# A four-stage model on one core: the next stage's weights, their preparations, the position shift and the turn of the expert loop

## The chip, the cores and the metric

One core of a Trainium2 chip runs one kernel. The metric is the device time of a run in microseconds (us), and the number given for a kernel is the median of its runs. The engines are PE (TensorE), DVE (VectorE), ACT (ScalarE), POOL (GpSimd) and SP (SyncE, which here only issues transfers).

## What is computed

A sequence model of two layers on x of 16 x 256 tokens by 128. Each stage is followed by x + stage(x) and a layer norm:

```python
x = _layernorm(x + _L0_attn_ref(x, ...))   # 16 heads of 64, j < i + 64; keys, queries, values from an MLP
x = _layernorm(x + _L0_ffn_ref(x, ...))    # 16 experts, 4 chosen per token
x = _layernorm(x + _L1_attn_ref(x, ...))   # 16 heads of 8; every weight W has a LoRA part A, B
x = _layernorm(x + _L1_ffn_ref(x, ...))    # a gated recurrence over 32 steps, as a scan over the batches
```

The expert stage and the LoRA part of the next one are what the change touches:

```python
logits = -sum((x - keys) ** 2) + x @ rw.T + rb
topv, topi = top_k(logits, 4); w = softmax(topv)
fused = sum(w * (gelu(x @ w1[e].T + b1[e]) @ w2[e].T + b2[e]) for e in topi)
y = x @ W.T + x @ A.T @ Blo.T / 16          # q, k, v and the output of the second attention
```

## The kernel before

The program gives each engine its own list of instructions, written out by hand; semaphores join them. It has four parts in time.

**First attention**, to 698 us. Batches 0 to 15 run through a loop (`batch_loop`, line 38: two turns written out, a `Fori` loop, the last turns written out). Towards a batch's end the router picks four experts for each token, and VectorE works out in which row of the DRAM array `xs` each token's copy goes: `posf_all` keeps the position of each of the 128 x 128 (token, choice) pairs, counted as if each expert had CAP rows. GpSimd scatters the tokens there (L493, eight indirect transfers a batch).

**The join.** When the last batch is counted, VectorE makes the plan: `NT` = 144 tiles of 128 rows, for each tile the expert and its first row. SP stores it and loads it back as one row, SP and ACT write zero rows behind each expert's tokens (`pad`, L353), PE multiplies the second bias out (L789). All four compute engines then meet at `a_done` (L507, L790 and their like; GpSimd counts itself there only after its scatters). Arrays of the first attention end here, and those of the later stages take their place in SBUF; `cw`, `lora_a`, `lora_b`, `gw`, `gu`, `gcol`, `bo1`, `bo2` are among these.

**Expert tiles**, from 712 us. [...] All five engines go round four tiles a turn. VectorE's order in a tile:

```python
e = expert_of(n + 2)       # a register read from the plan
need(dve, "hid_ready", 4 * n - 4)
weights_A(e, q)            # wA of tile n + 2
rows_T(n + 2, q)           # xgT of tile n + 2
v.tensor_tensor(yrow[:, m, :], DN[p % 2][:, 0:D], ...)   # tile n - 2
weights_B(e, q)            # wB of tile n + 2
```

Into the second written-out turn is put work for the later stages. SP issues eight loads after its first turn (L362). PE, ahead of tile 4, waits for all eight and multiplies the LoRA factors (L808); `add_lora` (L1312, L1314) adds them to `cw`; at tile 5 PE waits for that (`c_set`). After turn 1, `prepare` (L1319 to L1327) makes the small constants of the last stage on VectorE, and compares each position with the first row of each of the 16 experts (`shift`, 128 x 128 x 16). GpSimd waits for that compare (`plan_ready` 3), multiplies by `delta`, by how much an expert's rows move when the experts are packed without gaps (L534), adds the 16 up (L538, four sums of halves), adds the result to the positions (L541, L543), and goes on to clear and fill `qst`, `kst` and `v32` for the second attention (L511 to L553).

**Second attention with the recurrence**, from 1030 us, in one loop of three batches a turn; GpSimd gathers the rows of `ys` for it (L567).

Of the kernel before, what the change touches and what calls it, by code (L numbers as in the profile page):

```python
# [7 lines left out]
ACT = mybir.ActivationFunctionType  # L8
# [4 lines left out]
TT = N // 128  # L13
# [18 lines left out]
NT += -NT % 4  # L32
# [66 lines left out]
def build(nc, t, out):  # L99
    ctx = ExitStack()  # L100
    with ctx:
# [245 lines left out]
        def is_tile(i, p, off):  # L347
            return 0 <= 4 * i + p + off < NT if isinstance(i, int) else True
# [10 lines left out]
        def _(sp):  # L359
# [14 lines left out]

            sp.wait_ge(s["plan_ready"], 1)
# [31 lines left out]
            def body(i):  # L407
                for p in range(4):
                    n = 4 * i + p
                    if is_tile(i, p, 4):  # L410
                        load_rows(n + 4, p)
                    if p % 2 == 1 and is_tile(i, p, -5):
                        store_rows(n - 5, (p - 5) % 4)
                if isinstance(i, int) and i == 0:
                    for dst, src in ((cw, "cw"), (lora_a, "lora_a"), (lora_b, "lora_b"), (gw, "gw"), (gu, "gu"), (gcol, "gcol"),
                                     (bo1, "bo1"), (bo2, "bo2")):
                        load(dst, src, "cw_in")

            batch_loop(sp, 2, NT // 4 - 1, 2, body)
# [31 lines left out]
        def _(pool):  # L451
# [79 lines left out]
            pool.wait_ge(s["plan_ready"], 3)  # L531

            at = posf_all[:, :].rearrange("q (n o) -> q n o", o=1)
            g.tensor_tensor(shift[:, :, :], shift[:, :, :], delta[:, :].rearrange("q (o e) -> q o e", o=1).to_broadcast([128, npos, E]), ALU.mult)  # L534
            g.drain()
# [99 lines left out]
        def _(pe):  # L635
# [903 lines left out]
```

## Time and profile before

| what | us |
|---|---|
| three runs: 1596.56, 1600.42, 1598.92; median | 1598.92 |
| the profiled execution's own time | 1603.28 |
| its span | 1601.5 |
| PE busy in the span | 1305.1 (81%) |
| VectorE | 1059.0 (66%) |
| ScalarE | 960.6 (60%) |
| GpSimd | 785.4 (49%) |

Times in the profile count from the start of the span. "L818" is line 818 of the kernel as printed above. A row names the engine, the operation and its tiles as out<-in. Buffer numbers are left out, and an array seen through another one's memory has that one's name: `shift` shows as `qst`, `v32` as `v`. SPq, DVEq and POOLq are the engines' sequencers. The busy shares are averages over stages with different limits, so they don't tell what a change in one stage is worth; the idle time in brackets, and what ended it, do.

### The profile page before, as it was taken

The numbers are of one execution on the slowest core, as the hardware profiler recorded it, in microseconds if no ns is written. First come the engines' busy times: TensorE is split into PE (matmuls) and PEld (weight loads), VectorE is DVE, ScalarE is ACT, GpSimd is POOL, SyncE is SP. The second block draws the span as 40 slices with busy tenths as digits, with TensorE's granted clock in tenths as the row PEclk, the third lists the DMA queues.
The fourth block names the chain that finished last, engine by engine and source line by source line (L and its number), as shares of the span: only waits on it lengthen the run. The fifth ranks groups of instructions, "written<-read, shape, count | busy, mean of one in ns | idle before, by whom it ended". The sixth has DMA issues, their size and how long they took to land.

```text
span 1601.5 us, 37212 instructions
## 1 busy us (share of the span) xinstructions
PE 1305.1 (81%) x9486; PEld 975.0 (61%) x9486; DVE 1059.0 (66%) x3801; ACT 960.6 (60%) x2716; POOL 785.4 (49%) x898
## 2 busy tenths in 40 slices
PE   7999999999999999746799999703778777787871
PEld 3766666666666666436799999602445445455540
DVE  1677777777777777637766666414776767777646
ACT  5877777777777777423455555302565656556654
POOL 1567777777777777624400000276656655652003
PEclk9999999999999999958999999956898989889986
DMA  9100000000000000021122222123423223232101
GB/s 343 45 8 16 13 11 13 13 13 13 13 13 13 13 13 14 16 66 55 49 66 66 66 66 66 54 50 54 81 49 77 54 51 75 46 72 43 31 0 53
DMA packets 77063, 75.02 MB, mean 47 GB/s; under 512 B 10913, under 2 KB 66977, under 8 KB 75330
## 3 DMA queue, kind: packets, MB, share of 16 engines
q1 hardware_dynamic: 67506, 56.86, 13.9%
q0 software_dynamic: 8192, 16.79, 3.8%
q10 hardware_dynamic: 1296, 0.59, 0.1%
q8 instruction: 26, 0.43, 0.1%
q14 instruction: 43, 0.35, 0.1%
HBM read 46.87 MB, written 27.33 MB: 46 GB/s over the span
## 4 chain that ended last, share of the span: by engine, by line
PE 32%; issue 6%; ACT 5%; DVE 5%; POOL 3%; DVEq 2%; POOLq 2%; SPq 1%; DMA 0%; ACTq 0%
PE psum L818 8%; PE psum L829 7%; PE psum L862 3%; PE psum L851 3%; PE psum L926 3%; POOL yk L567 2%; ACT qst L1098 2%; PE psum L942 2%; PE psum L943 1%; ACT wall L1054 1%; ACT wall L1098 1%; DVE wA L1292 1%; PE psum L798 1%; PE psum L884 1%; DVEq L1431 1%
## 5 line engine op out<-in xcount | busy, mean ns | idle before, releaser
L503 POOL TENSOR_SCALAR P<-P,rinv 128x192 f32<-128x192 f32 (+1 forms) x384 | 308.8, 818 | 164.4 <-DVE rinv L1170 162.7
L1010 ACT ACTIVATE P<-shifted,least 128x192 f32<-128x192 f32 (+1 forms) x512 | 240.2, 471 | 126.4 <-DVE least L1156 125.1
L1044 ACT ACTIVATE hid<-psum,wA 128x128 f32<-128x128 f32 x576 | 164.9, 369 | 146.8 <-PE psum L818 146.7
L1368 DVE TENSOR_REDUCE mx<-psum 128x2 f32<-128x512 f32 x256 | 164.4, 685 | 82.6 <-PE psum L926 79.2
L1156 DVE CUSTOM_DVE_ANT_0 shifted<-psum,band 128x192 f32<-128x192 f32 (+1 forms) x512 | 168.7, 384 | 30.5 <-PE psum L695 30.2
L1054 ACT ACTIVATE wall<-psum 128x1024 f32<-128x1024 f32 x128 | 131.2, 1025 | 83.5 <-PE psum L851 81.2
L818 PE MATMUL psum<-xgT,wA 128*128 128x128 f32 x1152 | 162.3, 285 | 18.0 <-DVE xgT L1299 16.3
L818 PEld LDWEIGHTS psum<-xgT,wA 128*128 128x128 f32 x1152 | 143.7, 196 | 25.6 <-issue 25.3
L493 POOL DMA_INDIRECT xs<-x1c,pos x128 | 128.0, 1000 | 55.9 <-issue 28.2
L829 PE MATMUL psum<-wB,hid 128*128 128x128 f32 x1152 | 154.0, 278 | 0.0
L567 POOL DMA_INDIRECT yk<-ys,posc x128 | 123.7, 967 | 49.5 <-issue 37.1
L829 PEld LDWEIGHTS psum<-wB,hid 128*128 128x128 f32 x1152 | 142.1, 194 | 0.0
L731 PEld LDWEIGHTS psum<-ident,P 128*128 128x128 f32 x1024 | 116.8, 141 | 35.9 <-issue 28.9
L731 PE MATMUL psum<-ident,P 128*128 128x128 f32 x1024 | 134.1, 274 | 3.5 <-POOL P L503 1.4
L695 PE MATMUL psum<-kT,qT 64*128 64x192 f32 (+1 forms) x1024 | 131.5, 375 | 0.6 <-DVE least L1156 0.6
L1292 DVE COPY wA<-wall 128x516 f32 x144 | 75.4, 523 | 77.6 <-ACT hid L1044 67.4
L511 POOL MEMSET wall<- 128x2048 f32 x1 | 1.8, 1809 | 247.6 <-DVE wB L1295 247.6
L749 PE MATMUL psum<-PT,V 128*64 128x256 f32 (+1 forms) x1024 | 112.5, 362 | 0.7 <-DVE PT L1144 0.7
L695 PEld LDWEIGHTS psum<-kT,qT 64*128 64x128 f32 x1024 | 80.2, 186 | 38.5 <-issue 37.2
L1010 ACT ACTIVATION_READ_ACCUMULATOR P<-shifted,least 128x1 f32 x512 | 95.9, 187 | 0.0
L1295 DVE COPY wB<-wall 128x640 f32 x144 | 82.1, 570 | 19.8
L646 PE MATMUL psum<-hT,wg 128*128 (+1 forms) x256 | 88.9, 429 | 0.9 <-ACT kT L967 0.9
(247 smaller groups left out, 2671.8 us busy)
## 6 DMA issues: line engine op xcount, KB each, us to landing
xg<-xs SPq DMA_DIRECT2D x144, 64.0 KB, 1.8
ys<-yrow SPq DMA_DIRECT2D x72, 128.0 KB, 1.9
wall<-in_wall SPq DMA_DIRECT2D x1, 8232.0 KB, 36.6
qkd<-parts SPq DMA_DIRECT2D x32, 192.0 KB
qst<-qkd SPq DMA_DIRECT2D x66, 64.0 KB
wall<-qkd SPq DMA_DIRECT2D x35, 64.0 KB
kst<-qkd SPq DMA_DIRECT2D x11, 192.0 KB
hT<-in_xT SPq DMA_DIRECT2D x4, 512.0 KB, 6.1
```

Of the source, the lines that this page charges most:

```text
L493: nc.gpsimd.indirect_dma_start(out=xs, out_offset=bass.IndirectOffsetOnAxis(pos[:, k:k + 1], 0), in_=x1c[:, k // TOPK, :], in_offset=None) ...
L503: g.tensor_scalar(x, x, rinv[:, par, n:n + 1], None, ALU.mult).then_inc(s["pn_ready"], 1)
L567: g.indirect_dma_start(out=yk[:, n, :], out_offset=None, in_=ys, in_offset=bass.IndirectOffsetOnAxis(posc[:, n:n + 1], 0)).then_inc(s["yk_ ...
L695: last = mm(bk[:, c0:c0 + w], qT[64 * h:64 * h + 64, p, it * 128:(it + 1) * 128], kT[64 * h:64 * h + 64, p, 0:w], start=True, stop=True)
L731: last = nc.tensor.transpose(bk[:, c0:c0 + 128], P[:, par1, it, h, jt * 128:(jt + 1) * 128], ident[:, :])
L818: mm(UP[two][:, at:at + GT], wA[:, p, f * 128:(f + 1) * 128], xgT[:, p, :], start=True, stop=True).then_inc(s["up_mm"], 1)
L829: last = mm(DN[two][:, 0:D], hid[:, m, f, :], wB[:, m, f * D:(f + 1) * D], start=(f == 0), stop=(f == FC - 1))
L1010: last = sc.activation(P[:, par, it, h, 0:w], shifted[:, par, it, h, 0:w], ACT.Exp, scale=-1.0, bias=least[:, par, n:n + 1], accum_out=row ...
L1044: sc.activation(hid[:, p, f, :], UP[two][:, at:at + GT], ACT.Gelu, bias=wA[:, p, F + f:F + f + 1]).then_inc(s["hid_ready"], 1)
L1054: sc.activation(pc[:, p % 4, :, :, :].rearrange("q h j n -> q (h j n)"), ST, ACT.Exp, scale=SCALE1).then_inc(s["exps1"], 1)
L1156: v.tensor_tensor_reduce(out=shifted[:, par, it, h, 0:w], in0=bk[:, c0:c0 + w], in1=band[:, it, 0:w], scale=-SCALE0, scalar=3.0e38, op0=AL ...
L1368: v.tensor_reduce(out=mx[:, :, h], in_=SB[(par + 1 + h) % 3].rearrange("q (i n) -> q i n", i=TT), axis=mybir.AxisListType.X, op=ALU.max).t ...
```

## The change

It touches nothing that is computed. Five things:

- SP issues the eight loads right after the last output product of the first attention (`wo_mm`), ahead of the plan's store.
- PE multiplies the LoRA factors after the bias products, ahead of the join; VectorE adds them to `cw` after the plan, ahead of the join. No wait for them is left among the tiles.
- VectorE makes the last stage's constants right after the join, ahead of the first `wA`.
- The compare and the product of the position shift become 16 instructions on GpSimd, one per expert, each (position >= first row) x delta; GpSimd no longer waits for VectorE there.
- A turn of the expert loop has eight tiles (`TURN`) on every engine. `NT` stays 144. 16 tiles in front and 8 behind are written out in place of 8 and 4, and 15 turns are left of 33.

The diff, without the places where 4 becomes `TURN` in ACT's loop and in `is_tile`:

```diff
 DUMMY = E * CAP
 NT = (TOK * TOPK + E * (GT - 1)) // GT
-NT += -NT % 4
+TURN = 8
+NT += -NT % TURN
 ROWS = DUMMY + GT
...
+            sp.wait_ge(s["wo_mm"], PAIRS * B)
+            for dst, src in ((cw, "cw"), (lora_a, "lora_a"), (lora_b, "lora_b"), (gw, "gw"), (gu, "gu"), (gcol, "gcol"), (bo1, "bo1"), (bo2, "bo2")):
+                load(dst, src, "cw_in")
             sp.wait_ge(s["plan_ready"], 1)
...
             def body(i):
-                for p in range(4):
-                    n = 4 * i + p
+                for p in range(TURN):
+                    n = TURN * i + p
                     if is_tile(i, p, 4):
-                        load_rows(n + 4, p)
+                        load_rows(n + 4, p % 4)
                     if p % 2 == 1 and is_tile(i, p, -5):
                         store_rows(n - 5, (p - 5) % 4)
-                if isinstance(i, int) and i == 0:
-                    for dst, src in ((cw, "cw"), (lora_a, "lora_a"), (lora_b, "lora_b"), (gw, "gw"), (gu, "gu"), (gcol, "gcol"),
-                                     (bo1, "bo1"), (bo2, "bo2")):
-                        load(dst, src, "cw_in")
-
-            batch_loop(sp, 2, NT // 4 - 1, 2, body)
+
+            batch_loop(sp, 2, NT // TURN - 1, 2, body)
...
-            pool.wait_ge(s["plan_ready"], 3)
+            pool.wait_ge(s["plan_ready"], 2)
+            for e in range(E):
+                g.tensor_scalar(shift[:, :, e], posf_all[:, :], first_row[:, e:e + 1], delta[:, e:e + 1], ALU.is_ge, ALU.mult)
+            g.drain()
             at = posf_all[:, :].rearrange("q (n o) -> q n o", o=1)
-            g.tensor_tensor(shift[:, :, :], shift[:, :, :], delta[:, :].rearrange("q (o e) -> q o e", o=1).to_broadcast([128, npos, E]), ALU.mult)
-            g.drain()
...
+            pe.wait_ge(s["cw_in"], 128)
+            pe.wait_ge(s["pos_ready"], B)
+            for k in range(4):
+                last = mm(MIS[1][:, k * D:(k + 1) * D], lora_a[:, k, :], lora_b[:, k, :], start=True, stop=True)
+            last.then_inc(s["lora_mm"], 1)
...
             rows_in(0, 0, 16)
+            pe.wait_ge(s["c_set"], 1)
             rows_in(1, 1, 16)
             def tiles(i):
-                if isinstance(i, int) and i == 1:
-                    pe.wait_ge(s["cw_in"], 128)
-                    pe.wait_ge(s["xgT_ready"], 6)
-                    for k in range(4):
-                        last = mm(MIS[1][:, k * D:(k + 1) * D], lora_a[:, k, :], lora_b[:, k, :], start=True, stop=True)
-                    last.then_inc(s["lora_mm"], 1)
-                for p in range(4):
-                    n, two = 4 * i + p, p % 2
+                for p in range(TURN):
+                    n, two = TURN * i + p, p % 2
                     if is_tile(i, p, 0):
...
                             at = (f // 2) * 512 + (f % 2) * GT
-                            mm(UP[two][:, at:at + GT], wA[:, p, f * 128:(f + 1) * 128], xgT[:, p, :], start=True, stop=True).then_inc(s["up_mm"], 1)
-                    if isinstance(i, int) and i == 1 and p == 1:
-                        pe.wait_ge(s["c_set"], 1)
+                            mm(UP[two][:, at:at + GT], wA[:, p % 4, f * 128:(f + 1) * 128], xgT[:, p % 4, :], start=True, stop=True).then_inc(s["up_mm"], 1)
                     if is_tile(i, p, 2):
-                        rows_in(n + 2, (p + 2) % 4, 16 * (i + (p + 2) // 4) + 16)
+                        rows_in(n + 2, (p + 2) % 4, 16 * (i * (TURN // 4) + (p + 2) // 4) + 16)
...
+            dve.wait_ge(s["lora_mm"], 1)
+            for k in range(2):
+                v.scalar_tensor_tensor(cwqk[:, k, :].rearrange("q (d h) -> q h d", h=H1), MIS[1][:, k * D:(k + 1) * D].rearrange("q (h d) -> q h d", h=H1), LORA,
+                                       cw[:, k, :].rearrange("q (h d) -> q h d", h=H1), ALU.mult, ALU.add)
+            v.scalar_tensor_tensor(cw[:, 2:4, :], MIS[1][:, 2 * D:4 * D].rearrange("q (k d) -> q k d", k=2), LORA, cw[:, 2:4, :], ALU.mult, ALU.add)
+            v.drain().then_inc(s["c_set"], 1)
             dve.wait_ge(s["wall_in"], 16)
             dve.wait_ge(s["a_done"], 4)
+            v.tensor_copy(identb[:, :], ident[:, :])
+            v.tensor_scalar(gu[:, :, :], gu[:, :, :], 0.5, None, ALU.mult)
+            v.tensor_scalar(gcol[:, 0:2], gcol[:, 0:2], 0.5, None, ALU.mult)
+            v.memset(c2[:, :], 0.0)
+            v.drain()
+            v.tensor_scalar(c2[:, :], c2[:, :], gcol[:, 3:4], 2.0, ALU.add, ALU.mult).then_inc(s["scan_done"], 1)
...
-            def add_lora():
...
-                npos = B * TT * TOPK
-                v.tensor_tensor(shift[:, :, :], posf_all[:, :].rearrange("q (n o) -> q n o", o=1).to_broadcast([128, npos, E]),
-                                first_row[:, :].rearrange("q (o e) -> q o e", o=1).to_broadcast([128, npos, E]), ALU.is_ge).then_inc(s["plan_ready"], 1)
             def tiles(i):
-                for p in range(4):
-                    n, q = 4 * i + p, (p + 2) % 4
-                    if isinstance(i, int) and i == 1 and p == 0:
-                        add_lora()
+                for p in range(TURN):
+                    n, q = TURN * i + p, (p + 2) % 4
...
-                if isinstance(i, int) and i == 1:
-                    prepare()
-            batch_loop(dve, 2, NT // 4 - 1, 2, tiles)
+            batch_loop(dve, 2, NT // TURN - 1, 2, tiles)
```

How the order of instructions moves at three places (lines are those of each version). **PE at the join**, before: the bias products (the source is in `wall`) and then the first transposes of tiles (`xg`), with no LoRA product before tile 4.

```order
L789 MATMUL psum<-ident,wall 128x128 [waits wall_in]
L789 MATMUL psum<-ident,wall 128x128 x15
L798 MATMUL psum<-ident,xg 128x128 [waits xg_in0,a_done]
L798 MATMUL psum<-ident,xg 128x128 [waits xg_in1]
L818 MATMUL psum<-xgT,wA 128x128 [waits wA_ready,xgT_ready]
```

and now, on PE at the same place:

```order
L790 MATMUL psum<-ident,wall 128x128 x15
L794 MATMUL psum<-lora_b,lora_a 128x128 [waits pos_ready,cw_in]
L794 MATMUL psum<-lora_b,lora_a 128x128 x3
L804 MATMUL psum<-ident,xg 128x128 [waits xg_in0,a_done]
L804 MATMUL psum<-ident,xg 128x128 [waits xg_in1,c_set]
```

The four LoRA products stand ahead of the wait for `a_done`, and wait for the loads and for the last positions. **VectorE at the join**, before: the last value of the plan (`delta`), then the first expert's number and the first `wA`.

```order
L1279 COPY delta<-past 128x1
L1280 TENSOR_TENSOR delta<-past 128x15
L1289 TENSOR_LOAD plan [waits plan_in,a_done,wall_in]
L1289 ISA x2
L1292 ISA
L1292 COPY wA<-wall 128x516
```

and now, on VectorE at the same place (`c` is `c2`):

```order
L1278 TENSOR_TENSOR delta<-past 128x15
L1282 SCALAR_TENSOR_TENSOR cwqk<-psum,cw 128x16x8 [waits lora_mm]
L1282 SCALAR_TENSOR_TENSOR cwqk<-psum,cw 128x16x8
L1284 SCALAR_TENSOR_TENSOR cw<-psum,cw 128x256
L1290 CAST identb<-ident 128x128 [waits a_done,wall_in]
L1291 TENSOR_SCALAR gu<-gu 128x512
L1292 TENSOR_SCALAR gcol<-gcol 128x2
L1293 MEMSET c 128x256
L1295 TENSOR_SCALAR c<-c,gcol 128x256
L1300 TENSOR_LOAD plan [waits plan_in]
```

Three instructions came in ahead of the join and five between it and the first expert's number. **GpSimd after the join**, before, and now:

```order
L534 TENSOR_TENSOR qst<-qst,delta 128x2048 [waits scat,plan_ready,a_done]
L538 TENSOR_TENSOR qst<-qst 128x128x8
L538 TENSOR_TENSOR qst<-qst 128x128x4
L538 TENSOR_TENSOR qst<-qst 128x128x2
L538 TENSOR_TENSOR qst<-qst 128x128
```

```order
L534 TENSOR_SCALAR qst<-posf_all,first_row,delta 128x128 [waits scat,plan_ready,a_done]
L534 TENSOR_SCALAR qst<-posf_all,first_row,delta 128x128 x15
L539 TENSOR_TENSOR qst<-qst 128x128x8
L539 TENSOR_TENSOR qst<-qst 128x128x4
L539 TENSOR_TENSOR qst<-qst 128x128x2
```

One instruction over 2048 columns became 16 over 128, and what follows them is the same. The `plan_ready` it waits for is now the plan's own, no longer the compare's.

## Rows read from the trace of the kernel before

**Rows 1.** Busy time by engine in two stretches (start:end us, length, busy, PEclk, DMA)

```profile
698.00:712.60 14.60, 0.45 (x1) 0.18 (x1) 0.61 (x3) 0.00 (x0) 4.42 (x5) 0.55 0.37 110
...
738.07:780.82 42.75, 26.50 (x189) 25.09 (x188) 40.56 (x46) 12.91 (x44) 35.04 (x20) 0.88 0.12 34
```

**Rows 2.** In order of time (start us, us, engine line operation), tile 3 to tile 6

```profile
718.35 0.43 SPq L362 DMA_DIRECT2D cw<-in_cw  x1
...
718.93 1.06 PE L818 MATMUL psum<-xgT,wA 128*128 128x128 f32 x8
...
722.19 0.91 SPq L362 DMA_DIRECT2D bo<-in_bo  x2
...
725.08 2.07 PE L808 MATMUL psum<-lora_b,lora_a 16*128 16x128 f32 x8 [4.09 <-DMA bo<-in_bo]
...
727.26 0.59 DVE L1312 SCALAR_TENSOR_TENSOR cwqk<-psum,cw 128x128 f32<-128x128 f32 x2 [5.31 <-PE psum L808]
...
732.40 1.06 PE L818 MATMUL psum<-xgT,wA 128*128 128x128 f32 x8
```

**Rows 3.** In order of time, from the second turn's end to the end of GpSimd's chain

```profile
737.23 0.22 DVE L1319 CAST identb<-ident 128x128 bf16<-128x128 f32 x1
...
738.08 1.06 PE L818 MATMUL psum<-xgT,wA 128*128 128x128 f32 x8
...
738.48 2.28 DVE L1327 TENSOR_TENSOR qst<-posf_all,first_row 128x2048 f32<-128x2048 f32 x1
...
740.92 4.55 POOL L534 TENSOR_TENSOR qst<-qst,delta 128x2048 f32<-128x2048 f32 x1 [37.27 <-DVE qst L1327]
...
762.69 1.96 POOL L521 TENSOR_SCALAR_AFFINE_SELECT kst<-kst 24x2048 bf16<-24x2048 bf16 x1 [0.19 <-issue]
...
762.78 2.16 DVE L1292 COPY wA<-wall 128x516 f32 x1
...
778.35 0.36 POOL L553 MEMSET v<- 128x96 f32 x1
```

**Rows 4.** Up-projections over one turn, and VectorE's branches (durations ns min/median/max)

```profile
856.51 1.15 PE L818 MATMUL psum<-xgT,wA 128*128 128x128 f32 x8
...
860.43 1.08 PE L818 MATMUL psum<-xgT,wA 128*128 128x128 f32 x8
...
862.34 1.07 PE L818 MATMUL psum<-xgT,wA 128*128 128x128 f32 x8
...
864.48 1.15 PE L818 MATMUL psum<-xgT,wA 128*128 128x128 f32 x8
...
L43 DVEq COMPARE_BRANCH  x46: 50/56/72, 147.0 to 1021.8; - x46
```

**Rows 5.** The join: instructions in order of time, and two waits by line

```profile
674.87 1.13 PE L711 MATMUL psum<-OT,wo 128*128 128x256 f32 x4 [0.84 <-DVE OT L1148]
...
682.57 0.96 POOL L493 DMA_INDIRECT xs<-x1c,pos  x1 [0.30 <-issue]
...
690.77 6.28 PE L789 MATMUL psum<-ident,wall 128*128 128x128 f32 x32
...
707.51 0.43 DVE L1292 COPY wA<-wall 128x516 f32 x1 [9.33 <-issue]
...
712.62 0.29 DVE L1299 COPY xgT<-psum 128x128 f32<-128x128 f32 x1 [4.69 <-PE psum L798]
...
L507 POOLq DRAIN  x1: 1293/1293/1293, 705.1 to 705.1; - x1
...
L388 SPq EVENT_SEMAPHORE  x1: 1177/1177/1177, 707.6 to 707.6; - x1
```

**Rows 6.** Groups of GpSimd by line and shape (xcount | busy us, mean ns | idle)

```profile
L503 POOL TENSOR_SCALAR P<-P,rinv 128x192 f32<-128x192 f32 x256 | 196.0, 766 | 164.4 <-DVE rinv L1170 162.7
...
L503 POOL TENSOR_SCALAR P<-P,rinv 128x256 f32<-128x256 f32 x128 | 118.1, 923 | 0.0
...
L576 POOL TENSOR_TENSOR rstd<-ve,minus_half 128x4 f32<-128x4 f32 x12 | 12.5, 1043 | 44.5 <-DVE ve L86 44.4
```

More of the change, by code:

```diff
@@ L347, in is_tile @@
         def is_tile(i, p, off):
-            return 0 <= 4 * i + p + off < NT if isinstance(i, int) else True
+            return 0 <= TURN * i + p + off < NT if isinstance(i, int) else True
         def pad(eng, e):
@@ L830, in tiles @@
                         last.then_inc(s["dn_mm"], 1)
-            batch_loop(pe, 2, NT // 4 - 1, 2, tiles)
+            batch_loop(pe, 2, NT // TURN - 1, 2, tiles)
             pe.wait_ge(s["c_set"], 1)
@@ L1036, in tiles @@
             def tiles(i):
-                for p in range(4):
-                    n, two = 4 * i + p, p % 2
+                for p in range(TURN):
+                    n, two = TURN * i + p, p % 2
                     if is_tile(i, p, 0):
@@ L1043, in tiles @@
                             need(act, "up_mm", 4 * n + (2 * (f // 2) + 2))
-                            sc.activation(hid[:, p, f, :], UP[two][:, at:at + GT], ACT.Gelu, bias=wA[:, p, F + f:F + f + 1]).then_inc(s["hid_ready"], 1)
-            batch_loop(act, 2, NT // 4 - 1, 2, tiles)
+                            sc.activation(hid[:, p % 4, f, :], UP[two][:, at:at + GT], ACT.Gelu, bias=wA[:, p % 4, F + f:F + f + 1]).then_inc(s["hid_ready"], 1)
+            batch_loop(act, 2, NT // TURN - 1, 2, tiles)
             def attention(b, par):
@@ L1305, in _ @@
                 weights_B(first, n)
-            def add_lora():
-                dve.wait_ge(s["cw_in"], 128)
-                dve.wait_ge(s["lora_mm"], 1)
-                for k in range(2):
-                    v.scalar_tensor_tensor(cwqk[:, k, :].rearrange("q (d h) -> q h d", h=H1), MIS[1][:, k * D:(k + 1) * D].rearrange("q (h d) -> q h d", h=H1), LORA,
-                                           cw[:, k, :].rearrange("q (h d) -> q h d", h=H1), ALU.mult, ALU.add)
-                v.scalar_tensor_tensor(cw[:, 2:4, :], MIS[1][:, 2 * D:4 * D].rearrange("q (k d) -> q k d", k=2), LORA, cw[:, 2:4, :], ALU.mult, ALU.add)
-                v.drain().then_inc(s["c_set"], 1)
-            def prepare():
-                v.tensor_copy(identb[:, :], ident[:, :])
-                v.tensor_scalar(gu[:, :, :], gu[:, :, :], 0.5, None, ALU.mult)
-                v.tensor_scalar(gcol[:, 0:2], gcol[:, 0:2], 0.5, None, ALU.mult)
-                v.memset(c2[:, :], 0.0)
-                v.drain()
-                v.tensor_scalar(c2[:, :], c2[:, :], gcol[:, 3:4], 2.0, ALU.add, ALU.mult).then_inc(s["scan_done"], 1)
-                npos = B * TT * TOPK
-                v.tensor_tensor(shift[:, :, :], posf_all[:, :].rearrange("q (n o) -> q n o", o=1).to_broadcast([128, npos, E]),
-                                first_row[:, :].rearrange("q (o e) -> q o e", o=1).to_broadcast([128, npos, E]), ALU.is_ge).then_inc(s["plan_ready"], 1)
             def tiles(i):
-                for p in range(4):
-                    n, q = 4 * i + p, (p + 2) % 4
-                    if isinstance(i, int) and i == 1 and p == 0:
-                        add_lora()
+                for p in range(TURN):
+                    n, q = TURN * i + p, (p + 2) % 4
                     if is_tile(i, p, 2):
```

2 lines of the change are left out of this document (1 added, 1 removed).

## The prediction

> **What bounds the kernel now.** The stretch to read is the expert stage with the join ahead of it. I took the stages first [rows 1], then the instructions in order of time. From 698 to 712.6 us the join holds all engines: PE runs one matmul in 14.6 us and the clock averages 0.55. Then 144 tiles follow. Three things there set the time.
>
> First, a hole after tile 3 [rows 2]. Tile 3's up-projection starts at 718.93, and PE then waits for the eight loads that SP issues from 718.35 (the two bo, last, from 722.19 to 723.10). The LoRA products run only at 725.08, and tile 6 starts at 732.40: 13.47 us for three tiles.
>
> Second, GpSimd's chain [rows 3]. From VectorE's compare at 738.48 to GpSimd's last memset at 778.71, tiles are slow: 42.75 us [rows 1] for 11 tiles (the stage's two ends are put where up-projections start, the 1st and the 12th). The reader is to see why in one pair of rows: beside a GpSimd select of 1.96 us, the copy of wA takes 2.16 us, where it takes 0.43 us alone [rows 5]. The copy stands still until GpSimd's instruction is over, and a tile has two such copies.
>
> Third, the turn of the loop [rows 4]. In the quiet part after the chain, a turn takes 864.48 - 856.51 = 7.97 us, 1.99 us a tile. Inside it one tile takes 862.34 - 860.43 = 1.91 us, so four make 7.64 us, and 0.33 us is the turn's own. It falls on VectorE, whose branch, register work and read of the next expert's number delay the copies for which PE waits.
>
> **The change, part by part.**
>
> *The hole after tile 3.* Unrolled tiles are 1.89 us apart ((738.08 - 732.40) / 3 [rows 2, 3]). Without the loads and the products, three tiles take 5.68 us in place of 13.47: **-7.8 us**. What moves must be hidden elsewhere. The eight issues take SP 4.75 us (718.35 to 723.10 [rows 2]); they start when the last output product is done, at 674.87 + 1.13 = 676.0 [rows 5], so SP is free again near 681. Behind them in SP's queue stands the store of the plan, which VectorE can't have ready before the bias products' start at 690.77 [rows 5], since it counts the last batch first. What could suffer is GpSimd's scatter, with its last issue of that batch at 682.57 [rows 5], for which VectorE waits before it writes x1c: 0 to +1 us, taken as 0, since the loads are issued before. The four LoRA products cost PE 2.07 us [rows 2] after the bias products, which end at 690.77 + 6.28 = 697.05: PE is through at about 699.2, and VectorE's additions follow (two take 0.59 us [rows 2], a third comes) to about 700.2. The join opens only when GpSimd's drain ends, at 705.1 + 1.29 = 706.4 [rows 5]. Cover: 6 us; without it, 3 us would be paid.
>
> *Preparations ahead of tile 0.* VectorE's five small instructions take 738.48 - 737.23 = 1.25 us [rows 3]. They stand behind the join and push the first wA copy from 707.51 to about 708.8, or 711 if each waits for one of GpSimd's. PE cannot use it before xgT of tile 0, at 712.62, because SP first waits for the padding rows until 707.6 + 1.18 = 708.8 [rows 5]. Cost 0; up to +1 if the cover breaks.
>
> *Positions on GpSimd.* The compare of 2.28 us on VectorE and the product of 4.55 us on GpSimd go [rows 3]; 16 GpSimd instructions over 128 columns come. No row shows such a compare there. The nearest row is the same operation with a column as its scalar: 192 columns take 766 ns, 256 take 923 ns [rows 6], so 2.45 ns a column and, at 128, about 610 ns: 9.8 us in all. Bounds: 766 - 192 x 2.45 = 296 ns (4.7 us) is the part that doesn't depend on columns; upward 923 ns (14.8 us), if the second scalar costs as much as the columns saved. The far bound is the power, 1043 ns for 4 columns [rows 6]; I leave it to a rival, since it is another kind of function and the scale is the same kind of instruction. The Trainium skill speaks against this move: "GPSIMD Engine Reference", section "Performance versus the Vector engine", puts elementwise work on GpSimd at 1.96 times VectorE's time and keeps it on VectorE. By it the compare of 2.28 us would become 4.5 us, 5.3 us less than my 9.8; the end would be about 1 us earlier than below.
>
> *Where the chain now lies.* It starts at 706.4 in place of 738.48. The rest of it, from 745.47 (the product's end) to 778.71, is 33.2 us and stays. The small instructions end at 706.4 + 9.8 = 716.2, the rest at about 749.5. The 11 slow tiles cost 42.75 - 11 x 1.99 = 20.9 us, over 40.2 us of chain 0.52 us a microsecond. Afterwards the 33.2 us cost the same share, 17.3 us; of the small ones only 712.6 to 716.2 lies beside tiles, two tiles whose copies wait at most 0.6 us each, say 1.0 us. So 18.3 in place of 20.9: **-2.6 us**. Bounds: +3 (longer small instructions, and a clock that stays at 1.2 GHz under the holes; it averaged 0.88 in that stretch [rows 1]), and -6 (the first blocks fall on tiles that PE runs slowly anyway).
>
> *Eight tiles a turn.* 33 turns become 15: 18 x 0.33 = 5.9 us; 12 more tiles are unrolled at 1.89 instead of 1.91: 0.2 us. **-6.1 us**. Bounds -4 to -6.5: the branch row shows VectorE's at 50 to 72 ns over loops of different length [rows 4], so a longer body should cost nothing or little.
>
> Sum: -7.8 - 2.6 - 6.1 = -16.5 us. The profiled execution took 1603.3 us (span 1601.5), 4.4 above the median of 1598.9; against the median, 1582.4 us, so **1582 us**.
>
> **The rivals.**
>
> *A heavier front (18%).* The compare costs 923 ns or more, the holes of GpSimd's chain start while the clock is low, and it stays low through them. Then the second term is +3 and the loop gives 5: -7.8 + 3 - 5 = -9.8, about 1589 us. For it: the clock at 0.55 before tile 0. Against it: over the old chain it averaged 0.88.
>
> *A lighter front (12%).* The chain's blocks fall where PE is slow anyway and where the pipeline fills: -7.8 - 6 - 6.5 = -20.3, about 1578.5 us. For it: PE's first groups after the join run at the low clock. Against it: VectorE is then the later one all the same.
>
> *The longer turn saves nothing (5%).* The turn's cost grows with its body, so half the turns at twice the cost: -10.4, about 1588.5 us. Against it: the branch's 50 to 72 ns [rows 4]. The Trainium skill, "Runtime: NRT & Kernel Launch", section "Instruction fetch mechanics", says that a taken branch to code outside the window of two pages must fetch it first; a turn of eight tiles would do so if its code outgrew that window. No row shows such a stall.
>
> *Slower: the compare is dear (4%).* If one of the 16 took t us, the chain would be 16 x (t - 0.61) longer, all of it beside tiles that then take two instructions each. At t = 3: 38.2 us more, of which 1 - 1.91 / 6.2 is lost: +26.4, so about 1609 us, slower than before. It decides from t = 2.4 on (28.6 us x 0.62 = 17.7, more than the 16.5 won). For it: the power row, over 200 ns a column. Against it: the product ran at 4.55 us for 2048 columns [rows 3], 2.2 ns each, and the scale at 2.45.
>
> *The hole only moves (3%).* If the loads disturb the scatter and the LoRA products come after the drain, 6 us of the first term return: 1588 us; with the heavy front as well, about 1596 us, no change.
>
> **How the numbers follow.** The forecast has 58%. About 0.2%, 3.2 us, is what a measurement of this kernel can tell from no change. All cases but the dear compare and the double misfortune lie below 1595.7: faster 0.92, same 0.04, slower 0.04. The range takes in the unknowns of the forecast and both fronts, 1578.5 to 1589, with 2 us either way for the medians (the three runs before spread over 3.9): 1576 to 1591.
>
> **What would show it.** Tile 4's up-projection 1.9 to 4 us after tile 3's, and no LoRA row between them. GpSimd's 16 rows at about 0.6 us from 706 on, its last memset near 750, wA and wB copies of about 2 us between 722 and 750 and none later. Tile 0 still at 713. In the quiet part, eight tiles in 15.6 us. The tile stage 16.5 us shorter, and the second attention moved as a whole. Wrong it would be if tile 0 came late, if a compare took over 1 us, or if a turn took 15.9 us.

## The result and the profile after

The changed kernel takes 1579.85 us (median of four runs, 1579.33 to 1581.43), beside 1599.67 for the kernel before on the same chip (four runs, 1596.56 to 1603.67): a ratio of 0.988, 95% interval 0.986 to 0.990. Forecast were 1582.0 us and a range of 1576 to 1591. So it is 1.2% faster, and 2.2 us below the forecast. In what follows "the stage" is the time from the first to the last up-projection of the expert tiles.

A tile goes through the engines like this (lines of the changed kernel). SP loads its 128 rows into `xg`, PE transposes them (L804), and VectorE copies the result to `xgT` (L1310). VectorE also copies the expert's weights out of `wall` to `wA` (L1303) and `wB` (L1306). PE's up-projection (L818) reads `wA` and `xgT`, ScalarE applies the gelu (L1042), PE's down-projection (L827) reads `wB` two tiles later, VectorE adds the bias (`yrow`, L1331), and SP stores the rows.

| | before | after | change |
|---|---|---|---|
| profiled execution, its own time | 1603.28 | 1580.31 | -22.97 |
| span | 1601.5 | 1578.5 | -23.0 |
| start of tile 0's up-projection | 713.23 | 714.78 | +1.55 |
| the stage, first to last up-projection | 312.33 | 293.87 | -18.46 |
| from there to the end | 575.96 | 569.89 | -6.07 |

The last row has no edit in it (the experiments come back to it). Two stretches, the join and what follows to the end of GpSimd's chain, by engine with the columns of [rows 1]:

```profile
698.00:712.60 14.60, 1.18 (x9) 0.96 (x8) 3.54 (x15) 0.58 (x1) 10.15 (x12) 0.58 0.35 105
712.60:756.50 43.90, 31.64 (x224) 29.57 (x224) 39.08 (x54) 17.17 (x57) 41.11 (x30) 0.87 0.16 46
```

GpSimd works through both; before, it was idle in the first 28 us of the tiles. The second line answers to the second of [rows 1], where 11 tiles took 42.75 us; now 14 tiles take 41.74 us, from 714.78 to 756.52. The first six of these are quick, and the slow ones lie behind them. The join in order of time, against [rows 5]:

```profile
675.90 1.13 PE L712 MATMUL psum<-OT,wo 128*128 128x256 f32 x4 [0.84 <-DVE OT L1146]
...
677.06 0.34 SPq L363 DMA_DIRECT2D cw<-in_cw  x1
...
679.82 0.91 SPq L363 DMA_DIRECT2D bo<-in_bo  x2
...
691.91 6.18 PE L790 MATMUL psum<-ident,wall 128*128 128x128 f32 x32
...
698.02 1.15 PE L794 MATMUL psum<-lora_b,lora_a 16*128 16x128 f32 x8
...
699.25 0.58 DVE L1282 SCALAR_TENSOR_TENSOR cwqk<-psum,cw 128x128 f32<-128x128 f32 x2
...
707.58 0.23 DVE L1290 CAST identb<-ident 128x128 bf16<-128x128 f32 x1 [7.50 <-POOLq L507]
707.71 15.67 POOL L534 TENSOR_SCALAR qst<-posf_all,first_row,delta 128x128 f32<-128x128 f32 x16 [2.92 <-POOLq L507]
...
713.94 0.29 DVE L1310 COPY xgT<-psum 128x128 f32<-128x128 f32 x1 [3.82 <-PE psum L804]
...
714.78 1.94 PE L818 MATMUL psum<-xgT,wA 128*128 128x128 f32 x8
```

The reader is to see three things. The loads, the LoRA products and their additions are over at about 700.1, while VectorE waits 7.50 us for GpSimd's drain: they are covered. The whole join is about 1 us later than before, but so is its first row, the last output product (675.90 against 674.87), which comes ahead of every edit. And the 16 compares take 15.67 us, 0.98 us each, where 0.61 was forecast. (Their group in the profile has a mean of one of 1069 ns, since neighbours overlap.) Next, tiles 3 to 5 and the chain beside the tiles, against [rows 2, 3]:

```profile
720.49 1.06 PE L818 MATMUL psum<-xgT,wA 128*128 128x128 f32 x8
...
722.39 1.06 PE L818 MATMUL psum<-xgT,wA 128*128 128x128 f32 x8
...
724.28 1.06 PE L818 MATMUL psum<-xgT,wA 128*128 128x128 f32 x8
...
740.46 1.96 POOL L521 TENSOR_SCALAR_AFFINE_SELECT kst<-kst 24x2048 bf16<-24x2048 bf16 x1 [0.19 <-issue]
740.54 2.16 DVE L1303 COPY wA<-wall 128x516 f32 x1
...
742.95 1.16 PE L818 MATMUL psum<-xgT,wA 128*128 128x128 f32 x8 [2.15 <-DVE xgT L1310]
...
747.22 1.32 PE L818 MATMUL psum<-xgT,wA 128*128 128x128 f32 x8 [2.11 <-DVE xgT L1310]
...
756.11 0.36 POOL L554 MEMSET v<- 128x96 f32 x1
```

Tiles 3, 4 and 5 are 1.9 us apart: the hole is gone. Beside the selects a tile takes 747.22 - 742.95 = 4.27 us, as before, with the same 2.16 us copy. The chain ends at 756.47 where 749.5 was forecast. Last, a turn of the loop in the quiet part, the first up-projection of two turns in a row, against [rows 4]:

```profile
858.23 1.15 PE L818 MATMUL psum<-xgT,wA 128*128 128x128 f32 x8 [0.16 <-DVE xgT L1310]
...
873.94 1.15 PE L818 MATMUL psum<-xgT,wA 128*128 128x128 f32 x8 [0.16 <-DVE xgT L1310]
```

Eight tiles take 15.71 us. At 1.91 each they make 15.28, and 0.43 us is the turn's own, where 0.33 was forecast.

The stage's -18.46 us splits by the differences between up-projections: the three tiles of the hole -7.8, counted as what they took above 1.9 us each; the slow tiles beside GpSimd's chain, summed over what each takes above 1.9 us, 21.85 before and 15.24 after, -6.6; the same sum over the rest of the stage 11.0 and 6.94, -4.1.

### The profile page after: what moved, and what is told of

The parts are those of the page before. It is cut to its first block, busy times and chain, and to the rows that moved or that the text cites. A ratio compares the mean times of both kernels' runs of the same rounds, so it can differ in the third digit from the quotient of the medians.

```text
span 1578.5 us, 36791 instructions
## 1 busy us (share of the span) xinstructions
PE 1297.7 (82%) x9486; PEld 970.0 (61%) x9486; DVE 1055.8 (67%) x3800; ACT 959.6 (61%) x2716; POOL 796.1 (50%) x913
## 3 DMA queue, kind: packets, MB, share of 16 engines
q1 hardware_dynamic: 67506, 56.86, 14.1%
## 4 chain that ended last, share of the span: by engine, by line
PE 30%; issue 6%; DVE 6%; ACT 6%; DVEq 3%; POOL 2%; POOLq 1%; SPq 1%; DMA 0%; ACTq 0%
PE psum L818 7%; PE psum L827 6%; PE psum L860 4%; PE psum L849 3%; PE psum L924 3%; ACT qst L1096 2%; POOL yk L568 2%; PE psum L940 2%; PE psum L941 1%; ACT wall L1052 1%; DVE wA L1303 1%; ACT wall L1096 1%; PE psum L882 1%; PE psum L804 1%; DVE xgT L1310 1%
## 5 line engine op out<-in xcount | busy, mean ns | idle before, releaser
L1042 ACT ACTIVATE hid<-psum,wA 128x128 f32<-128x128 f32 x576 | 164.1, 368 | 129.2 <-PE psum L818 129.1
L818 PE MATMUL psum<-xgT,wA 128*128 128x128 f32 x1152 | 158.4, 281 | 13.0 <-DVE xgT L1310 12.3
L827 PE MATMUL psum<-wB,hid 128*128 128x128 f32 x1152 | 153.3, 277 | 0.0
L818 PEld LDWEIGHTS psum<-xgT,wA 128*128 128x128 f32 x1152 | 141.6, 193 | 17.4 <-DVE xgT L1310 12.1
L827 PEld LDWEIGHTS psum<-wB,hid 128*128 128x128 f32 x1152 | 141.4, 194 | 0.0
L732 PEld LDWEIGHTS psum<-ident,P 128*128 128x128 f32 x1024 | 116.8, 141 | 36.2 <-issue 29.3
L1303 DVE COPY wA<-wall 128x516 f32 x144 | 75.7, 526 | 64.1 <-ACT hid L1042 57.0
L1306 DVE COPY wB<-wall 128x640 f32 x144 | 79.1, 549 | 19.9
```

The lines of the kernel that those rows point to most:

```text
L732: last = nc.tensor.transpose(bk[:, c0:c0 + 128], P[:, par1, it, h, jt * 128:(jt + 1) * 128], ident[:, :])
L818: mm(UP[two][:, at:at + GT], wA[:, p % 4, f * 128:(f + 1) * 128], xgT[:, p % 4, :], start=True, stop=True).then_inc(s["up_mm"], 1)
L827: last = mm(DN[two][:, 0:D], hid[:, m, f, :], wB[:, m, f * D:(f + 1) * D], start=(f == 0), stop=(f == FC - 1))
L1042: sc.activation(hid[:, p % 4, f, :], UP[two][:, at:at + GT], ACT.Gelu, bias=wA[:, p % 4, F + f:F + f + 1]).then_inc(s["hid_ready"], 1)
```

## The experiments

Every kernel was measured beside the kernel before on the same chip. The stage of the kernel before was 312.33 and 313.93 us in its two profiles, 313.1 in the mean, against which the second column is taken.

| kernel | stage | less 313.1 | median less that of before | ratio, 95% interval |
|---|---|---|---|---|
| changed | 293.87 | -19.2 | -19.8 | 0.986 to 0.990 |
| changed, second time | 293.25 | -19.9 | -19.3 | 0.986 to 0.991 |
| changed, third time | 293.45 | -19.7 | -24.3 | 0.984 to 0.988 |
| changed, 4 tiles a turn | 298.49 | -14.6 | -22.1 | 0.985 to 0.991 |
| the same, second time | 299.10 | -14.0 | -16.6 | 0.988 to 0.991 |
| changed, 16 tiles a turn | 289.81 | -23.3 | -21.1 | 0.982 to 0.987 |
| before + early loads | 304.73 | -8.4 | -6.8 | 0.995 to 0.998 |
| before + compares on GpSimd | 306.29 | -6.8 | -9.4 | 0.993 to 0.996 |
| changed, GpSimd's chain in halves | 286.13 | -27.0 | -29.4 | 0.980 to 0.985 |
| changed, chain in quarters | 281.19 | -31.9 | -32.5 | 0.977 to 0.981 |
| quarters, 4 tiles a turn | 286.74 | -26.4 | -30.9 | 0.980 to 0.983 |
| quarters, 16 tiles a turn | 276.92 | -36.2 | -36.6 | 0.976 to 0.980 |

### The changed kernel once more

> The changed kernel once more. In the two profiles the expert stage (first to last up-projection) took 312.3 us before and 293.9 us changed, and from the last up-projection to the end it took 575.9 before and 569.8 changed, although nothing there was edited. Theory A (that part varies by itself): the stage is again 293.9 within 0.5 us, while the part behind it differs from 569.8 by more than 1 us. Rival B (the 6 us belong to the change, by where the gathers fall): 569.8 within 1 us again.

Measured: 1580.30 us (six runs, 1574.86 to 1583.44) beside 1599.55, and a stage of 293.25 us. The stage repeats within 0.7 us, a little more than the 0.5 expected, single runs of the whole within some 9. The part behind the stage took 567.96 us against 569.89, so it varies by more than 1 us with the same kernel: theory A.

### Four tiles a turn

```diff
-TURN = 8
+TURN = 4
```

> The changed kernel with four tiles a turn. By the two traces the quiet part costs 1.99 us a tile with four a turn and 1.964 with eight. Theory A: the loop gave 4 to 5 us, so this is 4 to 5 us slower than the changed kernel, the first 15 tiles unchanged. Rival B (a longer turn costs in proportion to its body): under 1 us slower.

Measured: a stage of 298.49 us, 5.2 longer than the changed kernel's measured beside it. A turn takes 7.97 us, as in the kernel before. But the median was 1577.48 us, 2.8 **below** the changed kernel's. By the stage theory A holds, by the median rival B. The pair was run again below.

### The loads and the LoRA products alone

```diff
 # the kernel before, with
+            sp.wait_ge(s["wo_mm"], PAIRS * B)
+            for dst, src in (...): load(dst, src, "cw_in")      # all eight
 # LoRA products after the bias products, add_lora ahead of the join, no c_set wait at tile 5
```

> The kernel before, with the eight loads, the LoRA products and their additions ahead of the join, all else as before. Theory A: the hole after tile 3 closes and nothing takes its place: 7.8 us faster than before. Rival B: the hole only moves (join later, or the chain's stall deeper): under 4 us faster.

Measured: 1592.76 beside 1599.55 us, ratio 0.9963, and a stage of 304.73: -7.6 us against the first profile of before, -8.4 against the mean of two. The hole is gone, and the slow tiles beside GpSimd's chain cost what they had cost. What is left of the second obstacle stands in this kernel's trace in order of time: VectorE's compare, GpSimd's product, and what tiles 10 and 11 wait for.

```profile
730.23 2.28 DVE L1324 TENSOR_TENSOR qst<-posf_all,first_row 128x2048 f32<-128x2048 f32 x1
...
732.66 4.55 POOL L533 TENSOR_TENSOR qst<-qst,delta 128x2048 f32<-128x2048 f32 x1 [29.67 <-DVE qst L1324]
733.17 0.97 PEld L816 LDWEIGHTS psum<-xgT,wA 128*128 128x128 f32 x8 [1.47 <-issue]
733.18 1.15 PE L816 MATMUL psum<-xgT,wA 128*128 128x128 f32 x8 [1.28 <-DVE xgT L1306]
...
733.39 4.18 DVE L1302 COPY wB<-wall 128x640 f32 x1
...
737.49 2.54 DVE L1299 COPY wA<-wall 128x516 f32 x1
...
740.36 2.07 PE L816 MATMUL psum<-xgT,wA 128*128 128x128 f32 x8 [5.03 <-DVE xgT L1306]
```

The compare puts VectorE back by 2.28 us. Beside the product of 4.55 us the copy of `wB` takes 4.18 us, and beside the first of the sums that follow the copy of `wA` takes 2.54. So the up-projections at 733.18 and 740.36 are 7.18 us apart (the one before 733.18 starts at 729.84). That place cost 6.7 us above two ordinary tiles (3.34 + 7.18 - 3.8). Most of it is the compare's and the product's; VectorE's small preparations, 1.25 us just ahead of the compare, and the first sum have a part in it that no run separates. The changed kernel has neither compare nor product there, and makes its preparations ahead of tile 0.

### The compares on GpSimd alone

```diff
 # the kernel before, with
-            pool.wait_ge(s["plan_ready"], 3)
+            pool.wait_ge(s["plan_ready"], 2)
+            for e in range(E): g.tensor_scalar(shift[:, :, e], ..., ALU.is_ge, ALU.mult)
 # VectorE's compare and GpSimd's product taken out
```

> The kernel before, with the 16 compares on GpSimd right after the join (and no compare on VectorE), the loads and the LoRA products left where they were. Theory A: GpSimd's compares lie beside the join and the hole, where no tile waits for a copy; the rest of its chain costs 15 us as in the changed kernel, less what falls in the hole: 6 to 9 us faster than before. Rival B (the chain costs the same 21 us wherever it lies, and the gain of the changed kernel came from the hole and the loop): under 3 us faster.

Measured: 1590.19 beside 1599.55 us, ratio 0.9945, and a stage of 306.29, so -6.0 or -6.8. The stage lies at the lower end of the 6 to 9 us expected and the median just above it, and rival B (under 3) is out. The prediction had given this part 2.6 us. Two things that the other edits change meet here. GpSimd's sums run while PE stands in the hole anyway, which costs nothing. And VectorE's small preparations, still behind turn 1, now fall among the selects:

```profile
743.18 1.96 POOL L521 TENSOR_SCALAR_AFFINE_SELECT kst<-kst 24x2048 bf16<-24x2048 bf16 x1 [0.19 <-issue]
743.26 1.96 DVE L1320 CAST identb<-ident 128x128 bf16<-128x128 f32 x1
...
745.48 1.91 DVE L1322 TENSOR_SCALAR gcol<-gcol 128x2 f32<-128x2 f32 x1
...
752.82 1.43 PE L819 MATMUL psum<-xgT,wA 128*128 128x128 f32 x5 [8.25 <-DVE xgT L1300]
```

Three of them take 1.9 us each, 1.91 us for two columns of `gcol`, where ahead of tile 0 in the changed kernel they take 0.15 to 0.43. The up-projection at 752.82 comes 11.35 us after the last one, 7.1 more than a slow tile. Moving the preparations ahead of tile 0 keeps this from happening once the chain starts early; what it is worth alone was not tried. The three parts alone, -8.4, -6.8 and -5.3 (four tiles a turn against eight), make -20.5; the whole is -19.6 in the mean of three profiles. They add up within 1 us. That is partly luck: the free sums and the dear preparations of this kernel pull in opposite directions.

### GpSimd's chain in quarters and in halves

What costs a slow tile its time: so much for each microsecond of chain, as the prediction had it, or the length of the single GpSimd instruction that a copy waits for? These kernels do the same work on the same elements in more instructions (in quarters 4 memsets become 16, six selects 24, and so on), so the chain gets longer.

```diff
             for r in ...:
-                g.affine_select(out=r, in_=r, ..., pattern=[[-1, H1 // 2], [0, N]], ...)
+                for c in pieces(N):          # four slices
+                    g.affine_select(out=r[:, :, c], in_=r[:, :, c], ..., pattern=[[-1, H1 // 2], [0, N // 4]], ...)
```

The memsets, the copy and the larger sums are cut likewise; the compares are not.

> The changed kernel with GpSimd's chain after the compares cut up: each clear, select, copy and sum of about 2 us becomes four instructions of a quarter of the columns (the clear of v32 six), the same work in all. Theory A (a copy on VectorE stands still until the GpSimd instruction under way is over, so what counts is how long ONE of them is): beside pieces of 0.3 to 0.7 us a tile takes 1.9 to 2.3 us as it did beside the 0.94 us compares, though the chain gets some us longer; the 15 us that the chain cost fall to 2 to 5, stage 281 to 284 us instead of 293.5. Rival B (the two engines share a bandwidth, the total counts): stage within 2 us of 293.5.

> The same with halves, pieces of about 1 us. Theory A: a tile's two copies wait at most 1 us each, about as beside the compares (0.94 us): stage 283 to 287 us. If the wait grows evenly with the piece's length, half of what the chain cost remains: about 286 us. Rival B: within 2 us of 293.5.

Measured: quarters 1562.46 us (five runs, 1560.49 to 1563.47) beside 1594.93, ratio 0.979; halves 1565.55 (1561.02 to 1572.24), 0.983. The stages are 281.19 and 286.13, both in the range of theory A, where rival B had 291.5 to 295.5. The groups by line and shape (count | busy us, mean ns) show why. First the changed kernel, the copies beside the compares (715 to 723.4) and beside whole instructions (727 to 756):

```profile
L1306 DVE COPY wB<-wall 128x640 f32 x5 | 2.9, 578 | 0.3
L1303 DVE COPY wA<-wall 128x516 f32 x5 | 2.5, 493 | 0.8 <-issue 0.5 <-ACT hid L1042 0.2
...
L1303 DVE COPY wA<-wall 128x516 f32 x8 | 14.9, 1863 | 0.0
L1306 DVE COPY wB<-wall 128x640 f32 x8 | 11.4, 1425 | 1.1
```

Then the same two copies with the chain in halves (730 to 750), with its selects:

```profile
L1313 DVE COPY wA<-wall 128x516 f32 x9 | 10.3, 1149 | 0.6 <-ACT hid L1052 0.3
L1316 DVE COPY wB<-wall 128x640 f32 x8 | 5.9, 739 | 1.1
...
L527 POOL TENSOR_SCALAR_AFFINE_SELECT kst<-kst 24x1024 bf16<-24x1024 bf16 x12 | 14.0, 1188 | 1.1 <-issue 1.1
```

and in quarters (737.8 to 760):

```profile
L1316 DVE COPY wB<-wall 128x640 f32 x11 | 8.6, 781 | 1.6
L1313 DVE COPY wA<-wall 128x516 f32 x10 | 7.1, 709 | 1.7 <-ACT hid L1052 1.6
...
L527 POOL TENSOR_SCALAR_AFFINE_SELECT kst<-kst 24x512 bf16<-24x512 bf16 x24 | 18.3, 794 | 1.1 <-issue 1.1
```

and last the kernel before with GpSimd idle (856 to 880), for the four alone:

```profile
L1295 DVE COPY wB<-wall 128x640 f32 x12 | 5.9, 494 | 1.7
L1292 DVE COPY wA<-wall 128x516 f32 x13 | 5.6, 430 | 7.1 <-ACT hid L1044 7.1
L1299 DVE COPY xgT<-psum 128x128 f32<-128x128 f32 x13 | 3.7, 284 | 0.0
L1345 DVE TENSOR_TENSOR yrow<-psum,wB 128x128 f32<-128x128 f32 x12 | 3.4, 280 | 0.0
```

Alone the four make 0.56 + 0.43 + 0.49 = 1.48 us a tile, where PE takes 1.9: a slack of 0.4 us. Beside the compares they make 0.56 + 0.49 + 0.58 = 1.63 us, 2.05 beside quarters, 2.45 beside halves and 3.85 beside whole instructions. The tiles measured 1.9, then 1.9 to 2.3, then 2.4 to 2.6, then mostly 4.1 to 4.3. So **a tile takes about the larger of PE's 1.9 us and VectorE's sum**: this is a rule read off these four cases, and at whole instructions the tiles are some 0.3 us longer than the sum. GpSimd instructions that lengthen the copies by less than the slack cost nothing. The selects' own time rose from 11.7 us in six to 18.3 us in 24, the chain ended 7.9 us later (764.34 against 756.47), and the stage was 12.7 us shorter than in the first profile of the changed kernel. A price for each microsecond of chain is refuted.

The Trainium skill, "SBUF — State Buffer", section "SBUF: two separate sides", says that VectorE and GpSimd share a pair of ports by an exclusive lock: a GpSimd instruction, or a VectorE one in a two-port mode or with two inputs from SBUF, gets the pair for the whole instruction, and the other one fully blocks. The trace agrees for the selects: the copy of `wA` beside one of 1.96 us took 2.16, beside one of 0.79 us some 0.71. It does not agree for the compares, if their rows in the profile are the time for which they hold the ports: they last 0.98 us, and the copies beside them took 0.49 and 0.58, 0.06 to 0.09 more than alone. Why was not tried. So a row's length alone doesn't tell what an instruction does to VectorE: 0.98 us of compare did less than 0.79 us of select. Cutting one kind of instruction into shorter ones is shown to help; whether a copy gets by because each piece is short, or in the part of each piece that doesn't depend on its size, these runs don't separate.

### Sixteen tiles a turn

```diff
-TURN = 8
+TURN = 16
```

> The changed kernel with 16 tiles a turn. The turn's own cost was 0.33 us with four tiles and 0.43 with eight (15.71 - 8 x 1.91). Theory A (it grows a little with the body and then no more): 6 turns left for 96 tiles, under 0.6 us each, stage 3 to 4 us shorter than 293.5. Rival B (it grows with the body's length, a fetch): over 1.5 us a turn, stage not shorter.

Measured: a stage of 289.81 us, 3.7 below the mean of the changed kernel's three, as theory A had it, and 1573.83 us (five runs, 1566.86 to 1576.01), ratio 0.9841. First up-projections of two turns in a row, with sixteen tiles:

```profile
854.01 1.15 PE L818 MATMUL psum<-xgT,wA 128*128 128x128 f32 x8 [0.17 <-DVE xgT L1310]
...
885.17 1.15 PE L818 MATMUL psum<-xgT,wA 128*128 128x128 f32 x8 [0.17 <-DVE xgT L1310]
```

and with four tiles, in the second four-tile kernel below:

```profile
851.32 1.15 PE L818 MATMUL psum<-xgT,wA 128*128 128x128 f32 x8
...
859.28 1.15 PE L818 MATMUL psum<-xgT,wA 128*128 128x128 f32 x8
```

31.16 and 7.96 us. Above 1.91 us a tile a turn costs 0.32 us with four tiles, 0.43 with eight and 0.60 with sixteen. The last is at the edge of the "under 0.6" expected. The cost grows with the body, but far more slowly than the body.

### The kernel before, for a second profile

> The kernel before, profiled once more, for what varies by itself. Theory A: the stage takes 312.3 us again within 0.5 us, its hole and its slow tiles at the same places, while the second attention's length (575.9 us from the last up-projection to the end) differs by more than 1 us. Rival B: it is 575.9 within 1 us, and so belongs to the version.

Measured: 1596.82 us, a stage of 313.93 us, tile 0 at 708.89. So a stage without any edit repeats within 1.6 us and not within the 0.5 expected; the hole cost 0.3 us more, the slow tiles 2.5 more, the rest 1.1 less. Tile 0's start, 713.23 in the first profile, moves by 4.3. The part behind the stage took 572.23 us against 575.96: theory A again.

### The turn once more, and with the chain in quarters

> The changed kernel with four tiles a turn, a second time. Open is why its first median was no worse than the changed kernel's although its tile stage was 5 us longer. Theory A (what the stage loses the run loses; the first median was the run to run variation of the second attention): stage from first to last up-projection 298 to 299 us against 293 to 294, and the median 4 to 5 us above the changed kernel's of the same call. Rival B (the second attention gives it back): the same stage, medians within 2 us of each other.

> The changed kernel again, as the neighbour of the four-tile version in the same call. Both theories: 0.988 of the kernel before, tile stage 293 to 294 us. Theory A: 4 to 5 us below the four-tile version; rival B: within 2 us of it.

Measured: four tiles a turn 1583.22 us (1581.06 to 1584.79), eight 1575.48 (1570.66 to 1579.24), beside 1599.79; stages of 299.10 and 293.45. Now the total follows, by more than the stage: 7.7 us against 5.7. Rival B, within 2 us, is out here. The two profiled executions differ by 14.1 us: 5.7 in the stage and 8.4 in the second attention, which no edit touches. From the last up-projection to the end it took 562.3 us in the profile of eight and 570.7 in that of four. Its three parts, in equal lengths but for the last (the columns are those of [rows 1]), first of eight tiles a turn, then of four:

```profile
1006.60:1200.00 193.40, 98.97 (x721) 62.21 (x720) 100.95 (x280) 70.23 (x99) 126.44 (x135) 0.73 0.29 61
...
1400.00:1568.90 168.90, 107.97 (x848) 71.65 (x848) 108.19 (x363) 96.97 (x155) 36.24 (x34) 0.84 0.16 37
```

```profile
1012.30:1205.70 193.40, 96.39 (x684) 61.04 (x683) 100.31 (x276) 68.09 (x94) 123.27 (x132) 0.71 0.31 60
...
1405.70:1583.00 177.30, 113.05 (x872) 74.53 (x864) 111.07 (x374) 100.97 (x159) 39.70 (x39) 0.83 0.16 35
```

In the same 193.4 us the second kernel is behind (684 matmuls against 721), at a granted clock of 0.71 against 0.73. Over all 14 profiles this part took between 562.3 and 576.0 us. Among the changed kernel and its variants neither the short nor the long ones go with a turn length: four tiles had 564.3, 570.7 and 565.0, eight 562.3 to 569.9. That, and not something given back, is the likely reason for the first four-tile median; it isn't shown. Why the clock differs from run to run stays open.

Something else does show in the 14. The four profiles of the kernel before and of the two built on it have 572.2 to 576.0 us, 573.5 in the mean; the ten of the changed kernel and its variants have 562.3 to 573.5, 567.6 in the mean. The medians point the same way with a smaller size: in the ten rows of the table that belong to the changed kernel, the median's difference is on average 2.0 us larger than the stage's. So some of the -6.07 of the first table may belong to the change after all; no run here shows how.

Then the two lengths with the chain in quarters:

> The changed kernel with GpSimd's long instructions of the chain cut into four and sixteen tiles a turn. The two gains lie at different tiles, so both theories expect the tile stage at 281.2 - 3.7 = 277.5 us. Theory A: the run is 3 to 4 us below the cut version with eight tiles, 0.976 to 0.978 of the kernel before. Rival B (turns are given back later): 0.979 to 0.980, as with eight.

> The same cut version with four tiles a turn. Stage 281.2 + 5 = 286 us. Theory A: about 8.5 us above the sixteen-tile version in the same call, 0.982 of the kernel before. Rival B: within 3 us of the sixteen-tile version.

Measured: stages of 276.92 and 286.74 us, within 1 us of the 277.5 and 286 expected, 9.8 apart; medians 1563.16 (1560.26 to 1568.94) and 1568.93 us (1563.84 to 1572.56), 5.8 apart, between theory A's 8.5 and rival B's 3. So a longer turn shows in the total in two of three pairs, and the stage shows it in each. A single median says where a kernel lies within some 4 us, and a stage of the profile within 1.6. In nine of the twelve rows of the table the stage's difference and the median's agree within 3 us, in two more within 5; only the first four-tile row is off by 7.5.

The quarters with eight tiles (ratio 0.9790) and with sixteen (0.9777) can't be told apart by total time, and both are well below both kernels of this case. The stage says sixteen is shorter.

## Why the prediction was right, and where its terms were not

**The hole, -7.8 us forecast.** Right in the changed profile (-7.8 above 1.9 us a tile, -7.5 if tiles 3 to 6 are compared directly, 13.47 against 5.98 us), -7.6 to -8.4 alone. The loads fit where the prediction put them: issued from 677.06 to 680.73, ahead of the plan's store, and the scatter's last issue of that batch (683.71 us) lay 7.8 us behind the output product's start, before 7.7. The LoRA products took 1.15 us instead of 2.07: the granted clock was 1.00 over them, behind 6.18 us of matmuls, and 0.50 (1.2 GHz) before, when PE had stood idle for 4 us. The cover of the drain was there, 7.50 us.

**Preparations, 0 forecast, up to +1.** Tile 0 started 1.55 us later in this profile, 1.0 of which stood before the join. Three profiles of the changed kernel had it at 714.78, 712.39 and 713.11, two of the kernel before at 713.23 and 708.89. No cost can be told from that spread.

**Positions on GpSimd, -2.6 forecast, -6.6 measured in the changed kernel.** This is the term that was mis-sized most, by 4.0 us. Here are two errors in the step, of opposite sign.

- The size: a compare with two columns as scalars costs 0.98 us, above even the upper bound of 0.92. The prediction had named "over 1 us" as what would prove it wrong; the group's mean of 1069 ns is over it, the 0.98 us from one start to the next just under. The chain ended 7 us later than forecast, 5.9 of them by the compares' length and 1.3 by their start at 707.71 in place of 706.4; the rest of the chain was 0.2 shorter. The Trainium skill's factor of 1.96, "GPSIMD Engine Reference", section "Performance versus the Vector engine", gave 4.5 us for the compare, by an estimate from one instruction over 2048 columns; the trace shows 15.7 us for compare and product together in 16 instructions over 128 columns, where they had taken 2.28 on VectorE and 4.55 on GpSimd.
- The rule of price, "0.52 us a microsecond" of chain. It was an average over long instructions and had no place for a threshold. By it the compares' extra 6 us would have cost 3; the quarters kernel shows what counts, by how much one instruction holds up one copy, against a slack of 0.4 us a tile. Of the 15.7 us of compares 7 lay ahead of tile 0, and over the 8.6 beside tiles a tile took 1.8 to 2.0 us: they cost next to nothing. What they replaced was the two dearest instructions of the chain, the 2.28 us on VectorE itself and the 4.55 us that blocked it; their place in the kernel with early loads cost 6.7 us.

**Eight tiles a turn, -6.1 forecast.** The mechanism was right, the size too large. With 0.43 instead of 0.33 us a turn, 33 x 0.33 - 15 x 0.43 + 0.2 = 4.6 us; the stage showed -5.3 in the mean of each kernel's profiles, and the split of the first profile -4.1 for all behind the slow tiles. The bound of -4 held. VectorE's branch row, on which "costs nothing or little" rested, doesn't hold the whole cost of a turn.

**The sum.** -16.5 forecast, -18.5 in the stage of the changed profile, -19.8 in the medians. By the split above, the second term gave 4.0 more than forecast and the third 2.0 less: -16.5 - 4.0 + 2.0 = -18.5. So the total came out near because two errors partly cancelled. What the medians have beyond that is within the spread of the stage (-19.6 in the mean of three profiles) and of the second attention.

**The rivals.** The heavier front came half true: the compare did cost more than 923 ns, but the clock averaged 0.87 over the slow stretch, and the term went the other way. The lighter front (-20.3, 1578.5 us) came nearest in its number, with -6 for the second term, though not by its reason: beside the compares VectorE had slack, and PE was slow only over the first tiles there (an up-projection took 1.94 us in tile 0 and 1.06 from tile 3 on). The longer turn did save: with four times the body its cost went from 0.32 to 0.60 us, without a jump. The Trainium skill, "Runtime: NRT & Kernel Launch", section "Instruction fetch mechanics", has a stall at a taken branch whose target lies outside a window of two pages; whether any of these branches left that window, no run here shows. The dear compare was not near: it decided from 2.4 us on. Of the hole that only moves, the double case was added up wrongly: -9.8 + 6 = -3.8 gives 1595.1 us, not about 1596, and this lies below the 1595.7 that it was said to pass.

## What to carry to other kernels

When GpSimd and VectorE disturb each other, ask how long a copy beside each kind of GpSimd instruction takes, not how long GpSimd is busy, and compare VectorE's work per tile, its wait included, with the time that the bounding engine leaves it. Long instructions of one kind are worth cutting up: cutting GpSimd's instructions up was worth 12 us here, two thirds of what the whole change brought. Price a step by what it takes out of the way as well as by what it adds. And compare kernels by the stage in the profile where the whole spreads more than the effect.

## What was not expected of the hardware

- GpSimd's compare of 128 x 128 with two columns as scalars: 0.98 us, more than the 256-column product with one column in [rows 6] (923 ns). Yet it held VectorE's copies up by under 0.1 us, where a select of 0.79 us held them up by 0.28.
- A quarter of a select costs 0.79 us where the whole costs 1.95, half of one 1.19: by an estimate from these three, some 0.4 us don't depend on the size, and even so the stage gained by paying them 18 more times.
- With quarters PE was busy 40.20 of the first 40.31 us of tiles and had a mean granted clock of 0.96; in the changed kernel it was busy 31.43 of the first 42.22 us, at 0.89.

```profile
709.69:750.00 40.31, 40.20 (x342) 39.82 (x341) 34.14 (x79) 25.08 (x85) 38.37 (x51) 0.96 0.23 66
```

```profile
714.78:757.00 42.22, 31.43 (x227) 29.60 (x227) 38.69 (x53) 17.17 (x57) 38.93 (x28) 0.89 0.16 45
```

The first line is the quarters kernel, the second the changed one; 342 matmuls against 227 in about the same time.
